# Attention heads: one PSUM bank of sums with two groups reopened in mid-head, four banks of scores, and fixed halves of rows

## The chip, the core and the metric

One core of a Trainium2 chip runs the whole program. Its engines are PE (matmuls; PEld is its weight load), DVE, ACT, POOL and SP; SP and ACT, and POOL for some, issue the DMAs. The metric is the device time in microseconds, lower is better.

## What is computed

Four layers in a row on 2048 tokens of 128 numbers. Each layer normalises, runs an attention and a feed-forward part, and adds their product to its input:

```python
xn = _layernorm(x, axis=-1)
s = _L0_attn_ref(xn, ...)            # layers 1, 2 and 3 likewise
g = _silu(_L0_ffn_ref(xn, ...))
x = x + s * g
```

The change touches the attentions of layers 0 and 3, with 16 heads of width 8 each. Layer 0's is full:

```python
scores = jnp.einsum('bhtd,bhsd->bhts', q, k) * scale
attn = jax.nn.softmax(scores, axis=-1)
out = jnp.einsum('bhts,bhsd->bhtd', attn, v)
```

Layer 3's is the same with rotated queries and keys and a causal mask (the reference takes 1e10 from a masked score, subtracts the row's maximum and takes the softmax).

## The kernel before

`attention_heads` runs both, `causal=False` for layer 0 (the full heads, some 50 to 750 us) and `causal=True` for layer 3 (the causal heads, some 1450 to 1922 us). Everything lies in stages; a stage ends with a barrier of all engines.

**Data of a head.** Queries and keys are split into three bf16 parts and stacked, with the products of parts that count, into 56 rows (`STK`) of `qs` and `ks`; this stack is loaded twice, into rows 0 to 55 and 64 to 119 (`HALF` is 64). Three rows more in each half (`qs`, rows 56 to 58 and 120 to 122) take the three parts of the negative row maxima, against rows of ones in `ks`. So a score matmul over 59 rows gives score minus maximum, and a maximum matmul over 56 rows gives the bare score. There are three sets of buffers (`ROUND`), head h in set h mod 3.

**Work of a head.** For a maximum, PE writes bare scores with queries on the partitions into a bank of `pM` (L742), and DVE reduces them (L880 in the full heads, two banks at once; L891 and, with the mask, L888 in the causal ones). When all are done, DVE makes `neg_max` (L897), its three parts are made (`split_max`, L610 to L616), PE transposes them (`turn`, L752) into a bank of `pS`, ACT copies them to `max_rows` (`keep_rows`, L836), and SP copies them into `qs` with one 4 KB DMA a part and half: six (`load_max_rows`, L643). For the result, PE writes scores with keys on the partitions into a bank of `pS` (L768; on the diagonal two 64-row mask matmuls follow, L771 and L772), ACT takes the exponential into `probs` (L855), and PE multiplies it by the values into 32-partition groups of `pO` (L786, the sums). ACT (full heads, L841) or DVE (causal, L910 and L911) copies `pO` to `ot`, and POOL stores it.

**Order.** It is written by hand, engine by engine. A head has units of four exponentials (`chunks`): 16 units in the full heads, 10 in the causal ones, where a unit pairs short and long rows of blocks. PE does the sums of unit u, and then the next four scores, each `RING` ahead of ACT, with the maxima of the next head (and of the one after) placed between them by `behind`. Scores wait for the bank that ACT freed `RING` chunks earlier, maxima for one of `FILLED` banks that DVE freed. Each matmul of L742 and L768 takes the other half of the rows than the one before it (`turns`), whatever it is:

```python
FILLED, RING, SUMS = (3, 3, 2) if causal else (4, 3, 1)
turns = itertools.cycle((0, HALF))
```

**Banks.** There are eight: full heads, four for maxima, three for scores, one for sums. Causal heads: three, three and two. Two, because in units 4 to 9 rows that lie behind the eighth or tenth are summed in groups that earlier units used for blocks 0 and 1 (`second`); those go to the second bank.

**Queues.** SP issues the loads of the head two on (`load_stacks`, ten DMAs, each behind a count of scores), then `load_max_rows`, then the row loads or clears of other work. At the start of a stage SP and ACT each load one half of the first keys (`load_first_keys`), SP behind DVE's first memset of ones and ACT behind its second. POOL sets the ones of the other two sets, two memsets each.

Of the kernel before, what the change touches and what calls it, by code (L numbers as in the profile page):

```python
# [18 lines left out]
P = 128  # L19
NT = T // P  # L20
BLK = 512
NB = T // BLK
# [73 lines left out]
def load_constants(nc, K, A):  # L96

    with Stage(nc, "load") as S:
# [17 lines left out]
        def _(dve):  # L116
# [9 lines left out]
            for to, at in ((slice(0, HALF), slice(HALF, P)), (slice(HALF, P), slice(0, HALF))):  # L126
                dve.tensor_copy(K.ident_swapped[to, :], K.ident[at, :]).then_inc(made, 1)
                dve.tensor_scalar(K.neg_below_swapped[to, :], masks[at, 1, :], NEG, None, ALU.mult).then_inc(made, 1)
# [388 lines left out]
def attention_heads(nc, K, layer, causal, scatter=None, spread=()):  # L517
# [11 lines left out]
    FILLED, RING, SUMS = (3, 3, 2) if causal else (4, 3, 1)  # L529
# [16 lines left out]
    with Stage(nc, f"heads{layer}") as S:  # L546
# [3 lines left out]
        ot = [S.sb(f"ot{i}", [P, SUMS, BLK]) for i in range(ROUND)]  # L550
# [10 lines left out]
        pO = S.ps("pO", [P, SUMS, BLK])  # L561
# [9 lines left out]
        last_stored = S.sem("last_stored")  # L571
        block = S.block()
# [3 lines left out]
        STORES = NB + len(SECOND)  # L576

# [27 lines left out]
        def split_max(queue, g):  # L605

            queue.wait_ge(splitting, 4 * g + 1)
            if g > 0:
                queue.wait_ge(rows_in, 32 * PARTS * g)
# [8 lines left out]
        def store_sums(queue, h, c, stored):  # L618
            for b in range(NB):
                queue.dma_start(K.head_out[h, :, b * BLK:(b + 1) * BLK], ot[c][b * 32:b * 32 + HD + 1, 0, :])\  # L620
                     .then_inc(stored, 16)
# [7 lines left out]
        def store_last(queue, turn):  # L629
            queue.wait_ge(ot_kept, LAST + 2)  # L630
            kept = ot[LAST % ROUND]
            pieces = [(K.head_out[LAST, :, b * BLK:(b + 1) * BLK], kept[b * 32:b * 32 + HD + 1, 0, :]) for b in range(NB)]
# [6 lines left out]
        def _(sp):  # L639
            def load_max_rows(c):  # L640
                for row in (STK, HALF + STK):
                    for a in range(PARTS):
                        sp.dma_start(qs[c % ROUND][row + a:row + a + 1, :].rearrange("o (t c) -> o t c", c=P),  # L643
                                     max_rows[a * NT:(a + 1) * NT, :]).then_inc(rows_in, 16)
# [16 lines left out]
            sp.wait_ge(ones_set[1], 2)  # L661
# [4 lines left out]
            sp.wait_ge(ones_set[2], 2)  # L666
# [12 lines left out]
        def _(pool):  # L679
# [7 lines left out]
            def one_head(p, c):  # L687
# [15 lines left out]
                if exists(p, c + 1):  # L703
                    pool.wait_ge(ot_kept, h + 2)
# [4 lines left out]
            for i in range(1, ROUND):  # L709
                for n, row in enumerate((HALF // 2, HALF + HALF // 2)):  # L710
                    pool.memset(ks[i][row:row + HALF // 2, :], 1.0).then_inc(ones_set[i], 1)
# [1906 lines left out]
```

## Time and profile before

| | us |
|---|---|
| median of 3 runs | 2002.25 |
| lowest, highest | 1996.25, 2002.73 |
| profiled execution | 1996.94 |
| its span, first to last instruction | 1995.1 |
| full heads, first maximum to last sums | 67 to 747 |
| causal heads, first maximum to last sums | 1466 to 1922 |

The page gives busy times over the whole span. The table by stretch gives them for a part of it; the granted clock 1.00 there is TensorE's upper level, 2.4 GHz, and 0.50 the lower, 1.2 GHz. The waits say who stood idle for whom, and the timeline gives rows in order: start, length, engine, line, what is written from what, how many in a row, and in brackets the idle time before them. Bursts of the same instruction are merged; their length is from the first start to the last end.

### The profile page before, as it was taken

To read this page: it belongs to the slowest core of one execution; us is meant where nothing else is said; L and a number is where in the kernel's file an instruction comes from. 1 tells how busy PE (TensorE), PEld (TensorE's weight loads), DVE (VectorE), ACT (ScalarE), POOL (GpSimd) and SP (SyncE) were. 2 spreads that over 40 slices of the span, in tenths; PEclk is the share of its full clock that TensorE was granted. 3 is DMA by queue.
4 is the path that set the end of the run, shared out by engine and by line. 5 is a ranking of instruction groups with operands and counts; after the bars stand their busy time and mean duration, and the time that the engine had idled before them with its cause. 6 is when DMAs were issued, how large, how long until landed. Compare 5 with 4: busy or idle time off the path is not lost. (4 is left out here: it accounts for less than half of the span.)

```text
span 1995.1 us, 29288 instructions
## 1 busy us (share of the span) xinstructions
PE 1650.5 (83%) x10105; PEld 666.2 (33%) x10105; DVE 1448.0 (73%) x2724; ACT 1112.2 (56%) x2262; POOL 313.7 (16%) x464
## 2 busy tenths in 40 slices
PE   3689999999999976799987986881659888999877
PEld 2212222222222214344444444771412222222246
DVE  5689999999999905855556056336768889999825
ACT  3258888888888881322212533342306666777744
POOL 0102100100010000000003345313012222111123
PEclk9779999999999997999987988886759999999989
DMA  4001111211110021063223587531501111111132
GB/s 132 32 20 63 66 51 45 73 61 46 46 61 32 4 47 66 5 127 94 93 105 112 154 285 252 184 114 49 182 33 46 47 41 45 42 45 52 32 78 69
DMA packets 80283, 156.07 MB, mean 78 GB/s; under 512 B 20476, under 2 KB 37756, under 8 KB 76440
## 3 DMA queue, kind: packets, MB, share of 16 engines
q1 hardware_dynamic: 65394, 123.90, 19.3%
q0 software_dynamic: 14384, 29.29, 4.9%
q8 instruction: 81, 1.33, 0.3%
q10 hardware_dynamic: 358, 1.01, 0.2%
q14 instruction: 66, 0.54, 0.1%
HBM read 104.33 MB, written 48.89 MB: 77 GB/s over the span
## 5 line engine op out<-in xcount | busy, mean ns | idle before, releaser
L855 ACT ACTIVATE heads_probs<-heads_pS 128x512 f32<-128x512 f32 (+3 forms) x1664 | 822.5, 578 | 217.9 <-PE heads_pS L768 195.5
L880 DVE TENSOR_REDUCE heads_run_max<-heads_pM 128x1 f32<-128x1024 f32 x512 | 601.0, 1219 | 37.0 <-PE heads_pM L742 29.1
L786 PE MATMUL heads_pO<-heads_probs,heads_vh 128*32 128x512 f32 (+2 forms) x3328 | 446.3, 583 | 2.1 <-ACT heads_probs L855 1.4
L768 PE MATMUL heads_pS<-heads_qs,heads_ks 59*128 59x512 bf16 (+3 forms) x1040 | 310.5, 371 | 30.4 <-ACT heads_probs L855 16.0
L742 PE MATMUL heads_pM<-heads_ks,heads_qs 56*128 56x512 bf16 (+3 forms) x1040 | 281.8, 380 | 17.3 <-DVE heads_run_max L891 7.1
L891 DVE TENSOR_REDUCE heads_run_max<-heads_pM 128x1 f32<-128x512 f32 x384 | 246.6, 684 | 18.9 <-PE heads_pM L742 17.8
L742 PE MATMUL heads_pM<-heads_ks,heads_q_first 56*128 56x512 bf16 x624 | 173.3, 397 | 44.1 <-DMA heads_ks<-k_parts_dram 25.8
L768 PE MATMUL heads_pS<-heads_q_first,heads_ks 59*128 59x512 bf16 x624 | 183.6, 376 | 23.8 <-ACT heads_probs L855 18.9
L768 PEld LDWEIGHTS heads_pS<-heads_qs,heads_ks 59*128 59x128 bf16 x1040 | 77.8, 94 | 321.6 <-ACT heads_probs L855 278.6
L888 DVE CUSTOM_DVE_ANT_0 heads_masked_out<-heads_pM,heads_mask_end 128x128 bf16<-128x128 f32 (+3 forms) x256 | 121.0, 486 | 28.5 <-PE heads_pM L742 26.1
L1616 DVE TENSOR_REDUCE second_row_max<-second_banks 128x1 f32<-128x2048 f32 (+15 forms) x16 | 20.7, 1291 | 156.0 <-PE second_banks L1574 77.5
L620 POOL DMA_DIRECT2D k_head_out_dram<-heads_ot x120 | 62.6, 529 | 365.3 <-DVE heads_ot L911 235.4
L1404 ACT ACTIVATE top_act_gate<-top_pG 128x512 f32<-128x512 f32 x68 | 40.6, 597 | 137.4 <-PE top_pU L1360 137.4
L768 PEld LDWEIGHTS heads_pS<-heads_q_first,heads_ks 59*128 59x128 bf16 x624 | 46.2, 94 | 201.8 <-ACT heads_probs L855 179.9
L1438 DVE TENSOR_TENSOR top_hidden<-top_act_gate,top_pU 128x512 f32<-128x512 f32 x68 | 46.7, 686 | 76.8 <-ACT top_act_gate L1404 76.8
L786 PEld LDWEIGHTS heads_pO<-heads_probs,heads_vh 128*32 128x32 f32 x3328 | 65.9, 108 | 96.3 <-issue 78.0
L742 PEld LDWEIGHTS heads_pM<-heads_ks,heads_qs 56*128 56x128 bf16 x1040 | 65.8, 94 | 96.3 <-DVE heads_run_max L880 62.6
L2115 POOL DMA_INDIRECT k_x_slots_dram<-k_xn,k_place_i x32 | 31.1, 971 | 390.3 <-DVE k_place_i L1984 361.5
L742 PEld LDWEIGHTS heads_pM<-heads_ks,heads_q_first 56*128 56x128 bf16 x624 | 39.7, 94 | 106.6 <-DVE heads_run_max L880 48.8
L610 POOL CAST heads_max_parts<-heads_neg_max 128x16 bf16<-128x16 f32 x16 | 3.1, 196 | 458.0 <-DVE heads_neg_max L897 458.0
L1359 PE MATMUL top_pG<-k_xnT,k_gate 128*128 128x512 f32 x128 | 67.3, 608 | 4.2 <-PEq L68 4.2
L1368 PE MATMUL top_pY<-top_hidden,k_down 128*128 128x512 f32 x128 | 65.7, 594 | 1.6 <-DVE top_hidden L1444 1.6
(384 smaller groups left out, 2139.5 us busy)
## 6 DMA issues: line engine op xcount, KB each, us to landing
top_weights<-k_comb_dram SPq DMA_DIRECT2D x128, 128.0 KB, 3.0
second_w<-in_L_W_dram SPq DMA_DIRECT2D x12, 1024.0 KB, 10.0
heads_ks<-k_parts_dram SPq DMA_DIRECT2D x124, 96.0 KB
k_hid_slots_dram<-k_zeros SPq DMA_DIRECT2D x8, 1152.0 KB, 4.5
k_h_slots_dram<-second_work SPq DMA_DIRECT2D x48, 192.0 KB
second_work<-k_hid_slots_dram SPq DMA_DIRECT2D x48, 192.0 KB
heads_qs<-k_parts_dram SPq DMA_DIRECT2D x40, 192.0 KB
k_parts_dram<-proj_part SPq DMA_DIRECT2D x12, 512.0 KB, 4.7
```

The source lines that it names most:

```text
L620: queue.dma_start(K.head_out[h, :, b * BLK:(b + 1) * BLK], ot[c][b * 32:b * 32 + HD + 1, 0, :])\
L742: mm = pe.matmul(pM[:, bank_of(c, j, k), 0:w], qs[c % ROUND][rows, i * P:(i + 1) * P], ks[c % ROUND][rows, b * BLK:b * BLK + w], start=Tru ...
L768: mm = pe.matmul(pS[:, slot, 0:c1 - c0], ks[c % ROUND][rows, u * P:(u + 1) * P], qs[c % ROUND][rows, c0:c1], start=True, stop=not diag)
L786: mm = pe.matmul(pO[k * 32:k * 32 + VW, int(second), o:BLK], vh[c][:, t, :], probs[u % 2][:, k * BLK + o:(k + 1) * BLK], start=first_chunk ...
L855: act.activation(probs[u % 2][:, k * BLK + c0 - b * BLK:(k + 1) * BLK], pS[:, slot, 0:c1 - c0], ACT.Exp)\
L880: dve.reduce_max(run_max[:, i, blocks[0][0] // 2:blocks[0][0] // 2 + 1], both.rearrange("p k c -> p (k c)"), AX.X).then_inc(taken, 2)
L888: dve.tensor_tensor_reduce(masked_out[:, i % TPB, 0:w], pM[:, bank, 0:w], mask_end[:, BLK - w:BLK], 1.0, LOWEST, ALU.add, ALU.max, run_max ...
L891: dve.reduce_max(run_max[:, i, b:b + 1], pM[:, bank, 0:w], AX.X).then_inc(taken, 1)
L1359: pe.matmul(pG[:, m % 2, :], gw, x, start=True, stop=True)
L1368: pe.matmul(pY[:, b % 2, :], w, hidden[:, m % 2, :], start=(n == 0), stop=(n == L1_J)).then_inc(downed, 1)
L1404: act.activation(act_gate[:, m % 2, :], pG[:, m % 2, :], ACT.Silu).then_inc(gated, 1)
L1438: mix = dve.tensor_tensor(hidden[:, m % 2, :], act_gate[:, m % 2, :], pU[:, m % 2, :], ALU.mult)
```

## The change

- **Banks, causal heads only.** `pO` has one bank, `pS` four (`RING` 4). The group of block 0 is complete when the sums of unit 3 are done, that of block 1 after unit 7. ACT copies each (32 partitions, 512 columns) to `ot` before it goes on with the third exponential of unit 4 and of unit 8; PE waits for that copy (`early_kept`) before the sums of that unit, which open the group again. At the head's end DVE copies the one bank with one instruction instead of two banks with two. POOL's stores also wait for `early_kept`.
- **Halves, both kinds of head.** `turns` is gone. Scores and masks use rows 0 to 63, maxima rows 64 to 127. So the maxima's rows are copied into the lower half alone: three DMAs instead of six. The stacks are still loaded into both halves.
- **Starts, both.** The upper half needs no ones: one DVE memset instead of two, two on POOL instead of four, and ACT's loads of the first keys wait for nothing.
- **The turn.** `TURN_AT` is `first_chunk[7] + RING`, so in the causal heads ACT copies the rows of the maxima behind chunk 31 instead of chunk 30.

```diff
-    FILLED, RING, SUMS = (3, 3, 2) if causal else (4, 3, 1)
+    FILLED, RING, KEPT = (3, 4, 2) if causal else (4, 3, 1)
...
+        reopened = {k: min(u for u, pieces in enumerate(units) if pieces[k][4]) for k, _ in SECOND}
+        EARLY = len(reopened)
+        keep_at = {first_chunk[u] + 2: k for k, u in reopened.items()}
...
         def load_first_keys(queue, turn):
             half = (0, HALF)[turn]
-            queue.wait_ge(ones_set[0], turn + 1)
+            if half == 0:
+                queue.wait_ge(ones_set[0], 1)
...
-                for row in (STK, HALF + STK):
-                    for a in range(PARTS):
-                        sp.dma_start(qs[c % ROUND][row + a:row + a + 1, :].rearrange("o (t c) -> o t c", c=P),
-                                     max_rows[a * NT:(a + 1) * NT, :]).then_inc(rows_in, 16)
+                for a in range(PARTS):
+                    sp.dma_start(qs[c % ROUND][STK + a:STK + a + 1, :].rearrange("o (t c) -> o t c", c=P),
+                                 max_rows[a * NT:(a + 1) * NT, :]).then_inc(rows_in, 16)
...
-                    at = next(turns)
-                    rows = slice(at, at + STK)
+                    rows = slice(HALF, HALF + STK)
...
-                at = next(turns)
-                rows, mask = slice(at, at + STK + PARTS), slice(at, at + HALF)
+                rows, mask = slice(0, STK + PARTS), slice(0, HALF)
...
+                opened = [k for k in reopened if reopened[k] <= u]
+                if u in reopened.values():
+                    pe.wait_ge(early_kept, EARLY * h + len(opened))
...
-                    mm = pe.matmul(pO[k * 32:k * 32 + VW, int(second), o:BLK], vh[c][:, t, :],
+                    mm = pe.matmul(pO[k * 32:k * 32 + VW, o:BLK], vh[c][:, t, :],
...
+                    if n in keep_at:
+                        rows = slice(keep_at[n] * 32, (keep_at[n] + 1) * 32)
+                        act.wait_ge(used, NU * h + 2 + reopened[keep_at[n]])
+                        act.activation(ot[c][rows, 0, :], pO[rows, :], ACT.Copy).then_inc(early_kept, 1)
...
-                        dve.tensor_copy(ot[c][:, 0, :], pO[:, 0, :])
-                        dve.tensor_copy(ot[c][0:2 * 32, 1, :], pO[0:2 * 32, 1, :]).then_inc(ot_kept, 1)
+                        dve.tensor_copy(ot[c][:, 1, :], pO[:, :]).then_inc(ot_kept, 1)
```

ACT in a causal head, from the exponentials of unit 3 to those of unit 8. `heads_probs<-heads_pS` is an exponential, `heads_max_rows` the copy of the maxima rows. Before:

```order
376 L855 ACTIVATE heads_probs<-heads_pS 128x512 x7
377 L855 ACTIVATE heads_probs<-heads_pS 128x384 x2
378 L855 ACTIVATE heads_probs<-heads_pS 128x512 x2
379 L855 ACTIVATE heads_probs<-heads_pS 128x256 x2
380 L855 ACTIVATE heads_probs<-heads_pS 128x512 x2
381 L855 ACTIVATE heads_probs<-heads_pS 128x128 x2
382 L855 ACTIVATE heads_probs<-heads_pS 128x512
383 L836 ACTIVATE heads_max_rows<-heads_pS 48x128
384 L855 ACTIVATE heads_probs<-heads_pS 128x512 x3
```

And after, in the same head:

```order
379 L865 ACTIVATE heads_probs<-heads_pS 128x512 x5
380 L858 ACTIVATE heads_ot<-heads_pO 32x512
381 L865 ACTIVATE heads_probs<-heads_pS 128x512 x2
382 L865 ACTIVATE heads_probs<-heads_pS 128x384 x2
383 L865 ACTIVATE heads_probs<-heads_pS 128x512 x2
384 L865 ACTIVATE heads_probs<-heads_pS 128x256 x2
385 L865 ACTIVATE heads_probs<-heads_pS 128x512 x2
386 L865 ACTIVATE heads_probs<-heads_pS 128x128 x2
387 L865 ACTIVATE heads_probs<-heads_pS 128x512 x2
388 L842 ACTIVATE heads_max_rows<-heads_pS 48x128
389 L865 ACTIVATE heads_probs<-heads_pS 128x512 x2
390 L858 ACTIVATE heads_ot<-heads_pO 32x512
```

The two copies of sums stand after the second exponential of units 4 and 8, and the copy of the maxima rows one exponential later than before.

PE in a causal head, from the last score ahead of the sums of unit 0 to the scores and maxima behind them (`heads_pO` the sums, `heads_pM` a maximum, `k_neg_below` the masks). Before:

```order
2416 L768 MATMUL heads_pS<-heads_qs,heads_ks 128x512
2417 L742 MATMUL heads_pM<-heads_ks,heads_qs 128x256
2418 L768 MATMUL heads_pS<-heads_qs,heads_ks 128x512
2419 L786 MATMUL heads_pO<-heads_probs,heads_vh 32x512 x4
2420 L768 MATMUL heads_pS<-heads_qs,heads_ks 128x512
2421 L742 MATMUL heads_pM<-heads_ks,heads_qs 128x512
2422 L768 MATMUL heads_pS<-heads_qs,heads_ks 128x256
2423 L771 MATMUL heads_pS<-k_neg_below,k_ident_b 128x128
2424 L772 MATMUL heads_pS<-k_neg_below_swapped,k_ident_swapped 128x128
```

And after, at the same place:

```order
2416 L771 MATMUL heads_pS<-heads_qs,heads_ks 128x512
2417 L746 MATMUL heads_pM<-heads_ks,heads_qs 128x256
2418 L771 MATMUL heads_pS<-heads_qs,heads_ks 128x512
2419 L792 MATMUL heads_pO<-heads_probs,heads_vh 32x512 x4
2420 L771 MATMUL heads_pS<-heads_qs,heads_ks 128x256
2421 L774 MATMUL heads_pS<-k_neg_below,k_ident_b 128x128
2422 L775 MATMUL heads_pS<-k_neg_below_low,k_ident_low 128x128
2423 L746 MATMUL heads_pM<-heads_ks,heads_qs 128x512
```

Every score stands one place further ahead of its sums; the maxima have kept their places.

## Rows read from the trace of the kernel before

**Rows 1.** The page: busy us, share of the span and instructions.

```profile
PE 1650.5 (83%) x10105; PEld 666.2 (33%) x10105; DVE 1448.0 (73%) x2724; ACT 1112.2 (56%) x2262; POOL 313.7 (16%) x464
```

**Rows 2.** Busy time by stretch: length, PE, PEld, DVE, ACT, POOL, clock, DMA.

```profile
150.00:390.00 240.00, 232.81 (x1567) 54.03 (x1559) 230.60 (x202) 205.86 (x403) 28.75 (x58) 1.00 0.16 56
...
1517.60:1708.15 190.55, 166.32 (x1353) 53.80 (x1351) 168.62 (x442) 130.27 (x287) 51.60 (x77) 0.98 0.15 45
...
1708.15:1889.95 181.80, 163.92 (x1348) 53.72 (x1346) 166.64 (x437) 129.51 (x287) 25.15 (x50) 1.00 0.15 43
```

**Rows 3.** Waits from 150 to 700 us; then DVE in order of time.

```profile
DVE heads_run_max L880 <- PE heads_pM L742: 11.9, 31, 0.8
...
317.75 2.36 DVE L880 TENSOR_REDUCE heads_run_max<-heads_pM 128x1 f32<-128x1024 f32 x2 [0.44 <-PE heads_pM L742]
...
501.16 2.36 DVE L880 TENSOR_REDUCE heads_run_max<-heads_pM 128x1 f32<-128x1024 f32 x2 [0.39 <-PE heads_pM L742]
...
633.74 19.09 DVE L880 TENSOR_REDUCE heads_run_max<-heads_pM 128x1 f32<-128x1024 f32 x16 [0.23 <-PE heads_pM L742]
```

**Rows 4.** SP's queue in order of time; the copies' landing.

```profile
309.85 4.28 SPq L643 DMA_DIRECT2D heads_qs<-heads_max_rows  x6
...
623.65 3.71 SPq L643 DMA_DIRECT2D heads_qs<-heads_max_rows  x6
...
1543.55 6.56 SPq L643 DMA_DIRECT2D heads_qs<-heads_max_rows  x6
...
1734.11 3.72 SPq L643 DMA_DIRECT2D heads_q_first<-heads_max_rows  x6
...
DMA to landing us min/median/max: 1.6/1.7/5.0
```

**Rows 5.** Starts of both stages in order of time; causal chain; page's DMA issues.

```profile
54.59 2.15 SPq L603 DMA_DIRECT2D heads_ks<-k_parts_dram  x3
...
56.85 1.97 ACTq L603 DMA_DIRECT2D heads_ks<-k_parts_dram  x3
...
67.16 1.04 PE L742 MATMUL heads_pM<-heads_ks,heads_q_first 56*128 56x512 bf16 x4 [4.81 <-DMA heads_ks<-k_parts_dram]
...
1457.99 7.59 DMA heads_ks<-k_parts_dram
...
top_weights<-k_comb_dram SPq DMA_DIRECT2D x128, 128.0 KB, 3.0
```

**Rows 6.** Head 15 of the causal stage, ACT and PE in order of time.

```profile
1904.45 2.06 ACT L855 ACTIVATE heads_probs<-heads_pS 128x512 f32<-128x512 f32 x4 [0.65 <-PE heads_pS L768]
...
1905.42 1.06 PE L786 MATMUL heads_pO<-heads_probs,heads_vh 128*32 128x128 f32 x8
...
1906.84 1.85 ACT L855 ACTIVATE heads_probs<-heads_pS 128x512 f32<-128x512 f32 x4 [0.33 <-PE heads_pS L768]
```

**Rows 7.** Copies of the sums by line: duration ns min/median/max.

```profile
L841 ACT ACTIVATE heads_ot<-heads_pO x16: 597/602/604, 159.6 to 746.1; 128x512 f32<-128x512 f32 x16
...
L911 DVE COPY heads_ot<-heads_pO x16: 672/673/674, 1525.9 to 1921.2; 64x512 f32<-64x512 f32 x16
```

**Rows 8.** A later causal head in order of time, PE and DVE.

```profile
1739.01 0.39 PE L768 MATMUL heads_pS<-heads_q_first,heads_ks 59*128 59x512 bf16 x1
...
1739.17 0.69 DVE L891 TENSOR_REDUCE heads_run_max<-heads_pM 128x1 f32<-128x512 f32 x1 [0.84 <-PE heads_pM L742]
```

**Rows 9.** The same head, matmuls in one half; page's weight loads of scores.

```profile
1736.82 0.27 PE L768 MATMUL heads_pS<-heads_qs,heads_ks 59*128 59x256 bf16 x1
...
1736.98 0.21 PE L772 MATMUL heads_pS<-k_neg_below_swapped,k_ident_swapped 64*128 64x128 bf16 x1
...
L768 PEld LDWEIGHTS heads_pS<-heads_qs,heads_ks 59*128 59x128 bf16 x1040 | 77.8, 94 | 321.6 <-ACT heads_probs L855 278.6
```

**Rows 10.** PE in the first full head; waits from 1517 to 1709 us.

```profile
103.19 0.61 PE L742 MATMUL heads_pM<-heads_ks,heads_q_first 56*128 56x512 bf16 x2 [0.52 <-DVE heads_run_max L880]
...
PE heads_pS L768 <- DMA heads_qs<-heads_max_rows: 5.7, 3, 2.7
```

More of the change, by code:

```diff
@@ L124, in _ @@
             dve.tensor_scalar(K.neg_below[:, :], masks[:, 1, :], NEG, None, ALU.mult).then_inc(made, 1)
-            for to, at in ((slice(0, HALF), slice(HALF, P)), (slice(HALF, P), slice(0, HALF))):
-                dve.tensor_copy(K.ident_swapped[to, :], K.ident[at, :]).then_inc(made, 1)
-                dve.tensor_scalar(K.neg_below_swapped[to, :], masks[at, 1, :], NEG, None, ALU.mult).then_inc(made, 1)
+            dve.tensor_copy(K.ident_low[:, :], K.ident[HALF:P, :]).then_inc(made, 1)
+            dve.tensor_scalar(K.neg_below_low[:, :], masks[HALF:P, 1, :], NEG, None, ALU.mult).then_inc(made, 1)
 class Norm:
@@ L549, in attention_heads @@
         vh = [S.sb(f"vh{i}", [P, NT, VW]) for i in range(ROUND)]
-        ot = [S.sb(f"ot{i}", [P, SUMS, BLK]) for i in range(ROUND)]
+        ot = [S.sb(f"ot{i}", [P, KEPT, BLK]) for i in range(ROUND)]
         probs = [S.sb(f"probs{i}", [P, T]) for i in range(2)]
@@ L576, in attention_heads, with sums_of_block @@
         STORES = NB + len(SECOND)
+        reopened = {k: min(u for u, pieces in enumerate(units) if pieces[k][4]) for k, _ in SECOND}
+        EARLY = len(reopened)
+        keep_at = {first_chunk[u] + 2: k for k, u in reopened.items()}
+        def sums_of_block(kept, b):
+            return kept[b * 32:b * 32 + HD + 1, 1 if causal and b not in reopened else 0, :]
         def every_head(one_head):
@@ L608, in split_max @@
             if g > 0:
[L609 removed]
+                queue.wait_ge(rows_in, 16 * PARTS * g)
             queue.tensor_copy(max_parts[:, 0, :], neg_max[:, :]).then_inc(splitting, 1)
@@ L629, in store_last @@
         def store_last(queue, turn):
+            queue.wait_ge(early_kept, EARLY * HEADS)
             queue.wait_ge(ot_kept, LAST + 2)
             kept = ot[LAST % ROUND]
-            pieces = [(K.head_out[LAST, :, b * BLK:(b + 1) * BLK], kept[b * 32:b * 32 + HD + 1, 0, :]) for b in range(NB)]
+            pieces = [(K.head_out[LAST, :, b * BLK:(b + 1) * BLK], sums_of_block(kept, b)) for b in range(NB)]
             pieces += [(K.head_more[LAST, :, (b - 2) * BLK:(b - 1) * BLK], kept[k * 32:k * 32 + HD + 1, 1, :])
@@ L709, in _ @@
             for i in range(1, ROUND):
-                for n, row in enumerate((HALF // 2, HALF + HALF // 2)):
-                    pool.memset(ks[i][row:row + HALF // 2, :], 1.0).then_inc(ones_set[i], 1)
-                    pool.wait_ge(ones_set[i], n + 1)
+                pool.memset(ks[i][HALF // 2:HALF, :], 1.0).then_inc(ones_set[i], 1)
+                pool.wait_ge(ones_set[i], 1)
             for i in range(ROUND):
@@ L725, in _ @@
         def _(pe):
-            turns = itertools.cycle((0, HALF))
             def bank_of(c, j, k):
@@ L771, in score_chunk @@
                     pe.matmul(pS[:, slot, 0:P], K.ident_b[mask, :], K.neg_below[mask, :], start=False, stop=False)
-                    mm = pe.matmul(pS[:, slot, 0:P], K.ident_swapped[mask, :], K.neg_below_swapped[mask, :], start=False,
+                    mm = pe.matmul(pS[:, slot, 0:P], K.ident_low[:, :], K.neg_below_low[:, :], start=False,
                                    stop=True)
@@ L914, in one_head @@
                             take(p, c + d, j)
-            for row in (HALF // 2, HALF + HALF // 2):
-                dve.memset(ks[0][row:row + HALF // 2, :], 1.0).then_inc(ones_set[0], 1)
+            dve.memset(ks[0][HALF // 2:HALF, :], 1.0).then_inc(ones_set[0], 1)
             if causal:
```

30 lines of the change are left out of this document (16 added, 14 removed).

## The prediction

> **What bounds the kernel now.** I read the page's busy shares first [rows 1], then the table by stage [rows 2], then the waits and the order of time inside the two stages that the change touches. Over the whole span no engine is the bound: PE, the busiest, has 83% [rows 1]. By stage it is clearer. In the full heads (150 to 699 us) DVE works 230.60 of 240 us [rows 2]: its 32 maxima a head run back to back, and what interrupts them is a group of short idles at each change of head, 11.9 us in 31 waits for maxima matmuls [rows 3]. In the causal heads from 1708 to 1890 us seven heads take 181.80 us, 25.97 each, and DVE is busy for 23.81 of them, PE for 23.42, ACT for 18.50 [rows 2]. No engine is full; the period comes from a loop. In head 15, where no maxima are made, ACT starts its four exponentials every 2.39 us (1904.45, 1906.84) and is idle 0.33 to 0.65 us before them [rows 6]: with three banks, the last score before the sums of a unit needs the bank that the unit's last exponential frees, the sums (1.06 us, at 1905.42) stand behind it in PE's order, and the first score behind the sums is what ACT then waits for.
>
> **Changes of head in the full heads.** SP issues six 4 KB copies of the maxima rows: 4.28 us where a code fetch or a clear is near, 3.71 us elsewhere, and the last needs 1.7 us to land [rows 4]. Behind the slow issue at 309.85 DVE is idle for 0.44 us at 317.75, and once more; behind the quick one at 623.65 there is one idle of 0.23 us, at 633.74 [rows 3, 4]: the excess follows the slow issue. Three copies need half the issue, about 1.9 us, at worst with the same excess of 1.3 us, 3.2 us: less than the 3.71 us that already do no harm. Taken off: 11.9, less two waits of 0.39 that lie in mid-head (one at 501.16 [rows 3]) and fourteen of 0.23 that stay, 7.9 us (7 to 9). SP's queue is only relieved: stack loads and clears stand behind the copies and move forward.
>
> **Starts of the two stages.** ACT's three loads of the first keys now wait for a second DVE memset: issued at 56.85 for 1.97 us, and PE starts 4.81 us late, at 67.16, on a load [rows 5]. In the causal stage ACT's last load is issued at 1457.99 and lands 7.59 us later [rows 5]. That wait is gone, so ACT's loads leave at the stage's start and SP's three, issued from 54.59 to 56.74 [rows 5], land last. No row has their landing. Bounds: 3.0 us (128 KB, a quiet time) and 7.59 us (three queues' worth in flight) [rows 5], so the first maximum at 59.7 to 64.3 instead of 67.16: 2.8 to 7.4 us. With half of the traffic already gone I take 5 us, and the same for the causal stage, whose start has the same shape: 10 us (6 to 13). Four memsets fewer on POOL and two on DVE are beside this wait.
>
> **Fixed halves.** Scores now always stream from rows 0 to 63, maxima from 64 to 127, and two neighbours in one half can't overlap. In the steady loops the neighbours are nearly always one of each; where the full heads have M M and S S next to each other, the pairs that start together (S M, M S, S M, M S) are those of before, so nothing is lost. The first head of a stage is all maxima: a pair takes 0.61 us with PE idle 0.52 us before it [rows 10]; one behind the other adds 512 columns at the low clock (1.2 GHz, 0.43 us), which leaves almost no slack in DVE's 1.13 us. I add 1.7 us for both first heads (0 to 3). In head 15 scores alone follow each other, 0.21 us each, inside the time of ACT's exponentials: nothing.
>
> The row for back-to-back matmuls of one half: a 256-column score starts at 1736.82, and the second mask matmul behind it, after 384 columns of the same half, at 1736.98 [rows 9]: 0.16 us, the streaming alone at 2.4 GHz. The Trainium skill (TensorE: Matmul & The Clock Gate, Part 3: Packing small matmuls) says that a weight load overlaps a running matmul only when it goes to other rows of the array; by that every such neighbour would cost its load, and this trace does not agree.
>
> **Causal heads, the copied rows.** The same six copies took 6.56 us at 1543.55 and 3.72 us in the later heads [rows 4]; PE waited up to 2.7 us for them [rows 10]. The seven heads from 1517.60 to 1708.15 took 190.55 us, 8.8 us over seven times 25.97 [rows 2]. Three copies halve that issue, but the turn now stands one exponential later, and what fetches SP's code can still hit it. I take 5.9 us of the 8.8 (3 to 8.8). In the later heads SP's issue begins at 1734.11 and PE takes the next head's first score at 1739.01 [rows 4, 8], 4.9 us against 3.1 + 1.7: just in time. After: 1.3 + 1.7 = 3.0 us against about 3.9 (0.6 less for the later turn, 0.4 for a faster loop).
>
> **Causal heads, the loop.** With four banks one more score stands ahead of the sums, so ACT has four exponentials (2.06 us) to do while PE does 0.4 + 1.0 + 0.33 us: ACT no longer waits and the loop of 2.39 opens. PE then needs 1.06 us of sums, four times 0.21 us of score and maximum side by side, 0.17 us of masks (16 a head, two each) and about 0.1 us of hand-over: 2.2 us a unit, 22 a head. DVE drops its second copy (0.67 us, [rows 7]): 23.81 - 0.67 = 23.1 us a head. That is the floor. Of DVE's 2.2 idle us a head some stay, since the maxima are spread unevenly: three behind unit 7 and five behind unit 8, where it waits 0.84 us now [rows 8]; I leave 1.0.
>
> Then the two added copies, each a new wait: ACT stops after two exponentials of the unit until the sums of the unit before are done, copies 32 rows (nearest row: 128 rows of the same 512 columns, 0.602 us [rows 7]; between nothing and that), and only then come the last two exponentials, behind which PE waits. Sums to sums: 1.0 + 0.1 + 0.5 + 1.1 + 0.2 = 2.9 us instead of 2.3. Behind PE's wait stand scores and maxima, behind those DVE, with three banks (1.8 us) in hand. So 0 to 0.8 us each; I take 0.35 for both, since most falls under DVE's work. Period 23.1 + 1.0 + 0.35 = 24.5 us, 1.47 less. Fifteen heads: 22 us. Bounds: 23.1 (43 us) and 25.97 (nothing). Head 15 gains 0.2 a unit and pays two copies: nothing.
>
> **Sum.** 7.9 + 10 - 1.7 + 5.9 + 22 = 44 us. The profiled execution took 1996.94 us (span 1995.1), so 1953; the median of the three runs is 2002.25, 5.3 above it, so 1958.
>
> **Rivals.**
> 1. The loop opens fully. DVE runs at its floor of 23.1 us: 21 us more, 1937. For it: DVE is the fullest engine. Against: the three-maxima unit.
> 2. The mid-head copies take it back. Each costs PE its full 0.6 to 0.8 us and DVE follows, so the period stays at 25.9: 1980. For it: PE at 22 of 24.5 us has little to catch up with, and one copy falls right behind the thin unit 7. Against: three banks of maxima.
> 3. Loads bound the faster loop. The keys for two heads on, and the rows, land as late as before while PE asks earlier: period 25.2, 1958 + 10 = 1968. For it: the margins above are within a microsecond.
> 4. The slower side: weight loads in one half are exposed. There are 720 such neighbours in the full heads (three a unit) and about 150 in the causal ones. At a load's 0.094 us each [rows 9] they cost 82 us: 1958 + 82 = 2040. It decides from 0.05 us a neighbour. Against it stand the 0.16 us of [rows 9]. The Trainium skill's rule above would have it so.
> 5. The change doesn't do what it says at the starts, because the loads landing last are SP's own and take 7.59 us: 6 us less, 1964; inside the range of the forecast.
>
> **Chances.** Forecast 0.45 with 5 (1948 to 1968), rival 1 0.15, rival 2 0.2, rival 3 0.15, rival 4 0.05. The range takes in rivals 1 to 3 and the bounds of the load landing: 1936 to 1984. A measurement of this kernel can tell 0.3% (6 us) from no change: faster 0.92, same 0.04, slower 0.04.
>
> **What would show it.** In the full heads: DVE idle 0.23 at each change of head, period near 38.7 us. At the starts: first maxima near 62 and 1461. In the causal heads: turns 24.5 us apart, ACT's wait before its fours gone except at the two copies, DVE busy 95% of a head. Wrong would be: a turn distance of 25.9 with PE waiting for the copied rows of the sums (rival 2); PE waiting on key loads (3); scores of one half 0.3 us apart instead of 0.21 (4).

## The result and the profile after

The changed kernel takes 1989.46 us (median of 5 runs, 1981.55 to 1991.0) against 2002.25 for the kernel before beside it: ratio 0.9937 (0.9917 to 0.9957). It is faster, by 0.6% where the prediction had 2.2%, and lies above its range (1936 to 1984 us). The span of the profiled executions fell from 1995.1 to 1989.2 us.

The table by stretch of the changed kernel, from 150 to 390 us in the full heads and for two stretches of the causal ones, six and seven heads from one copy of maxima rows to another (length, PE, PEld, DVE, ACT, POOL, granted clock, DMA share, GB/s):

```profile
150.00:390.00 240.00, 239.56 (x1601) 57.28 (x1598) 235.10 (x206) 210.14 (x412) 28.45 (x56) 1.00 0.17 61
1536.73:1698.35 161.62, 141.28 (x1160) 44.89 (x1159) 141.59 (x373) 116.81 (x258) 44.36 (x66) 1.00 0.15 45
1698.35:1885.80 187.45, 164.48 (x1349) 52.14 (x1348) 163.90 (x432) 136.29 (x302) 25.26 (x50) 1.00 0.14 41
```

The full heads are what was forecast: DVE busy 235.10 of 240 us, 230.60 before [rows 2]. The causal heads are not: seven take 187.45 us, **26.78 each**, where they took 25.97 [rows 2] and 24.5 was forecast. DVE and PE have 23.4 and 23.5 us of work in them, so both stand idle longer than before.

Some of the waits of the changed kernel from 1517 to 1880 us (us in total, times, longest):

```profile
ACT heads_probs L865 <- PE heads_pS L775: 59.0, 68, 1.3
...
ACT heads_ot L858 <- PE heads_pO L792: 27.1, 27, 1.3
...
DVE heads_run_max L901 <- PE heads_pM L746: 19.0, 13, 2.2
```

The second row is new: ACT waits at each mid-head copy for the sums of the unit before, 1.0 us on average. The third was 13.0 us in 16 waits, the longest 0.8, in the same view of the kernel before. In order of time, ACT in one causal head (start, length, and in brackets the idle time before; `heads_ot` is the mid-head copy):

```profile
1645.08 1.08 ACT L865 ACTIVATE heads_probs<-heads_pS 128x512 f32<-128x512 f32 x2
1647.46 0.59 ACT L858 ACTIVATE heads_ot<-heads_pO 32x512 f32<-32x512 f32 x1 [1.29 <-PE heads_pO L792]
1648.07 2.40 ACT L865 ACTIVATE heads_probs<-heads_pS 128x384 f32<-128x384 f32 x6
...
1661.69 1.08 ACT L865 ACTIVATE heads_probs<-heads_pS 128x512 f32<-128x512 f32 x2 [0.87 <-PE heads_pS L775]
1663.52 0.59 ACT L858 ACTIVATE heads_ot<-heads_pO 32x512 f32<-32x512 f32 x1 [0.75 <-PE heads_pO L792]
1664.02 4.49 ACT L865 ACTIVATE heads_probs<-heads_pS 128x512 f32<-128x512 f32 x10
```

Units 8 and 4: two exponentials, 1.29 and 0.75 us idle, the copy of 0.59 us, then the other exponentials. The third exponential starts 3.0 and 2.3 us after the first instead of 1.0, and PE's later scores of the next unit, which need the banks that the last two exponentials free, and the sums stand behind them.

The starts and the changes of head of the changed kernel, the same rows as [rows 3 to 5]:

```profile
59.62 1.02 PE L746 MATMUL heads_pM<-heads_ks,heads_q_first 56*128 56x512 bf16 x4 [1.72 <-DMA heads_ks<-k_parts_dram]
...
652.73 1.82 SPq L649 DMA_DIRECT2D heads_qs<-heads_max_rows  x3
...
DVE heads_run_max L890 <- PE heads_pM L746: 3.3, 14, 0.2
...
1458.10 1.79 PE L746 MATMUL heads_pM<-heads_ks,heads_q_first 56*128 56x128 bf16 x6 [16.35 <-DMA heads_ks<-k_parts_dram]
```

The first maximum comes at 59.62 us instead of 67.16, and fourteen changes of head (the third row, from 150 to 735 us) hold one idle of at most 0.2 us each. The two profiles differ by 5.9 us:

| stretch | before, us | after, us | difference |
|---|---|---|---|
| to the first full maximum | 67.16 | 59.62 | -7.5 |
| maxima of the first full head | 39.40 | 45.45 | +6.1 |
| the second full head | 42.51 | 43.29 | +0.8 |
| fourteen further full heads | 549.81 | 540.75 | -9.1 |
| from there to the first causal maximum | 766.84 | 768.99 | +2.2 |
| first causal head, to the first copy of rows | 22.79 | 22.78 | 0.0 |
| fifteen causal heads | 401.14 | 404.92 | +3.8 |
| last causal head and the rest | 105.45 | 103.40 | -2.1 |

### The profile page after: what moved, and what is told of

It is laid out like the page before. It is cut to its first block and busy times, and to the rows that moved or that the text cites. A ratio compares the mean times of both kernels' runs of the same rounds, so it can differ in the third digit from the quotient of the medians.

```text
span 1989.2 us, 29248 instructions
## 1 busy us (share of the span) xinstructions
PE 1678.2 (84%) x10105; PEld 672.3 (34%) x10105; DVE 1437.9 (72%) x2704; ACT 1127.3 (57%) x2294; POOL 306.7 (15%) x460
## 5 line engine op out<-in xcount | busy, mean ns | idle before, releaser
L746 PE MATMUL heads_pM<-heads_ks,heads_qs 56*128 56x512 bf16 (+3 forms) x1040 | 319.0, 379 | 19.9 <-DVE heads_run_max L901 9.6
L746 PE MATMUL heads_pM<-heads_ks,heads_q_first 56*128 56x512 bf16 x624 | 201.4, 397 | 33.8 <-DMA heads_ks<-k_parts_dram 18.1
L771 PE MATMUL heads_pS<-heads_q_first,heads_ks 59*128 59x512 bf16 x624 | 189.9, 377 | 13.2 <-ACT heads_probs L865 11.8
L898 DVE CUSTOM_DVE_ANT_0 heads_masked_out<-heads_pM,heads_mask_end 128x128 bf16<-128x128 f32 (+3 forms) x256 | 121.2, 487 | 25.9 <-PE heads_pM L746 21.6
L1870 PE MATMUL second_banks<-second_w,second_hT 128*96 128x128 f32 x384 | 56.1, 294 | 15.6 <-ACT second_hT L1921 8.6
```

The costliest lines, as they stand in the source:

```text
L746: mm = pe.matmul(pM[:, bank_of(c, j, k), 0:w], qs[c % ROUND][rows, i * P:(i + 1) * P], ks[c % ROUND][rows, b * BLK:b * BLK + w], start=Tru ...
L771: mm = pe.matmul(pS[:, slot, 0:c1 - c0], ks[c % ROUND][rows, u * P:(u + 1) * P], qs[c % ROUND][rows, c0:c1], start=True, stop=not diag)
L898: dve.tensor_tensor_reduce(masked_out[:, i % TPB, 0:w], pM[:, bank, 0:w], mask_end[:, BLK - w:BLK], 1.0, LOWEST, ALU.add, ALU.max, run_max ...
L1870: pe.matmul(pY[0:R, n % 2, 0:D], hT[:, n % 2, f, :], w[:, e, f * D:(f + 1) * D], start=(f == 0), stop=False)
```

## The experiments

Two questions: what made the causal heads slower than before, and what took the start's gain back. Theory A puts the first down to the two mid-head copies and the waits around them; B to the fixed halves; C to the end of a head. All experiments were measured later, each beside the kernel before, which takes 1946 to 1948 us there: the stages between the two kinds of heads are some 50 us shorter (672.2 us in one more profile of it instead of 719.6). The record names two chips for them, 12 (`copy_latest`, `dve_copies`, `again`, `later_alt`) and 0 (the others). So they are compared by ratio, and by the causal period: the mean distance of the copies of maxima rows in the late heads, a head with a stall left out. For one and the same kernel the period agrees in all measurements (25.97 and 25.96 us before, 26.78 and 26.79 after).

**1. `two_banks`: all of the change but the banks** (and what hangs on them: the mid-head copies, the later turn, DVE's one copy instead of two)**.**

```diff
-    FILLED, RING, KEPT = (3, 4, 2) if causal else (4, 3, 1)
+    FILLED, RING, KEPT = (3, 3, 2) if causal else (4, 3, 1)
...
-        pO = S.ps("pO", [P, BLK])
+        pO = S.ps("pO", [P, KEPT, BLK])
...
-        keep_at = {first_chunk[u] + 2: k for k, u in reopened.items()}
+        keep_at = {}
...
```

> The changed kernel with the sums as before: two banks of sums and three of scores in the causal heads, no copy in mid-head, two copies by DVE at a head's end. Fixed halves, three copies of rows and the early loads stay. In the changed kernel the maxima rows of the causal heads are copied every 26.8 us (26.0 in the kernel before). Theory A, the two mid-head copies and their waits cost it: here the period is the loop of the kernel before, 25.9 us, without its stalls behind six row copies, so 15 x 0.9 = 13.5 us less than the changed kernel, some of it given back in head 15 (2.8 us): 1979 us. Theory B, PE loses by the fixed halves in the loop: the period stays at 26.8 or above, 1990 us or more. Theory C, the end of a head (turn, rows, first scores) sets the period whatever the banks: 26.0 to 26.8.

Measured: 1927.42 us, ratio 0.9892 (0.9872 to 0.9912), where the changed kernel had 0.9937. Period 25.95 us against 25.97. Fixed halves cost nothing in the loop, and B falls: the new period comes with the banks. C's lower bound of 26.0 is too near to 25.95 to be ruled out by this run alone; the next one does that.

**2. `no_copies`: the changed kernel without ACT's copies and PE's waits for them.**

```diff
-        keep_at = {first_chunk[u] + 2: k for k, u in reopened.items()}
+        keep_at = {}
...
-                if u in reopened.values():
-                    pe.wait_ge(early_kept, EARLY * h + len(opened))
```

> The changed kernel without the two mid-head copies and PE's waits for them: the sums of blocks 0 and 1 of the causal heads are therefore overwritten and wrong, all else is as in the changed kernel (one bank of sums, four of scores). Theory A (the copies and their waits cost the gain of the fourth bank): period 24.5 us, 15 x 2.3 = 34 us less than the changed kernel, 1955 us. Theory B (fixed halves): period 26 at least, 1977 us. Theory C (end of head): 26.0 to 26.8 here too, 1980 to 1989.

Measured: 1900.94 us, ratio 0.9774 (0.9750 to 0.9799), period 24.91. This kernel has the same end of head as the changed one, later turn included, so C falls. Seven of its heads in the table by stretch:

```profile
1603.29:1777.64 174.35, 161.74 (x1353) 52.35 (x1352) 163.12 (x435) 129.47 (x287) 29.27 (x54) 1.00 0.16 49
```

The fourth bank (with the later turn and DVE's one copy less) is worth 25.95 - 24.91 = 1.04 us a head, and the mid-head copies with their waits cost 26.79 - 24.91 = 1.9. DVE works 23.3 of the 24.91 us: 1.6 us idle stay where the prediction left 1.0.

Where the 1.9 us go shows in PE's rows from the sums of unit 7 to those of unit 8, first in the changed kernel, with the copy of 1647.46 between them, then without copies:

```profile
1646.35 1.06 PE L792 MATMUL heads_pO<-heads_probs,heads_vh 128*32 128x128 f32 x8
...
1648.62 0.23 PE L771 MATMUL heads_pS<-heads_qs,heads_ks 59*128 59x128 bf16 x1 [0.66 <-ACT heads_probs L865]
...
1649.42 1.06 PE L792 MATMUL heads_pO<-heads_probs,heads_vh 128*32 128x512 f32 x8
```

```profile
1629.79 1.07 PE L789 MATMUL heads_pO<-heads_probs,heads_vh 128*32 128x128 f32 x8
...
1631.72 1.06 PE L789 MATMUL heads_pO<-heads_probs,heads_vh 128*32 128x512 f32 x8
```

From sums to sums it is 3.07 us with the copy and 1.93 without; from unit 3 to unit 4 it is 3.04 and 2.32. The two differences, 1.14 and 0.72, add up to the 1.9 us: nothing of them is hidden. The third exponential comes behind the copy, PE waits 0.66 us for the bank that it frees before it writes its third score, and the maxima, the last score and the sums stand behind that one. DVE then waits 1.4 us for the maxima behind the sums of unit 8, where it waits 0.5 us without copies (the 2.2 of the view further up is from one early head).

**3. `copies_ring3`: the changed kernel with three banks of scores.**

```diff
-    FILLED, RING, KEPT = (3, 4, 2) if causal else (4, 3, 1)
+    FILLED, RING, KEPT = (3, 3, 2) if causal else (4, 3, 1)
```

> The changed kernel with three banks of scores instead of four; one bank of sums and the two mid-head copies stay (one bank of PSUM unused). Theory A: the fourth bank is worth 25.9 - 24.5 = 1.4 us a head and the copies cost 2.3 us, so without it the period is 28.2 us, 21 us more than the changed kernel: 2010 us. If the mid-head wait makes the fourth bank worthless, since PE refills it only behind the same sums, the period stays at 26.8: 1989 us. Theory C: also 26.8.

Measured: 1942.0 us, ratio 0.9979 (0.9967 to 0.9991), period 27.18. So with the copies in that place the fourth bank is worth only 0.4 us a head, not 1.04. The distance from sums to sums over a copy is 3.03 and 3.04 us here and 3.07 and 3.04 with four banks, where without copies it is 2.34 and 2.40 with three banks (`two_banks`) and 1.93 and 2.32 with four: the copy sets it, and what the bank opens in these two units is lost. Neither number forecast (28.2 or 26.8) was met.

**4 and 5. `copy_later` and `copy_latest`: the same copies behind the third and behind the fourth exponential.** One number is changed, to 3 in `copy_later` and to 4 in `copy_latest`:

```diff
-        keep_at = {first_chunk[u] + 2: k for k, u in reopened.items()}
+        keep_at = {first_chunk[u] + 4: k for k, u in reopened.items()}
```

> The changed kernel with each mid-head copy one exponential later: behind the third exponential of units 4 and 8 instead of the second. ACT waited 1.3 us for the sums of the unit before ahead of each copy; with one exponential (0.52 us) more in front the wait is 0.8 us, and PE gets the copy no later. Theory A: up to 2 x 0.5 = 1.0 us a head less, period 25.8 to 26.3, 1975 to 1982 us. If PE then waits as much longer for the copy as ACT waits less, nothing changes: 1989 us. Theories B and C: nothing, 1989 us.

> The changed kernel with each mid-head copy behind all four exponentials of units 4 and 8 (second in the changed kernel, third gave 25.92 us a head). ACT finds the sums done and waits no more (0.6 us less for each than behind the third); but PE's sums of the unit come only after the copy, 0.6 us later. Theory: each costs about its own 0.6 us in front of PE's sums, 24.91 + 1.2 = 26.1 us a head, between the other two; 1918 us. If PE has room there, 25.3.

Measured: behind the third 1915.13 us, ratio 0.9839 (0.9821 to 0.9857), period 25.92; behind the fourth 1903.45 us, ratio **0.9777** (0.9758 to 0.9795), period **24.91**, the same as with no copy at all. The miss on the last is over 1 us a head. ACT of that kernel in order of time, units 4 and 8:

```profile
1646.51 2.06 ACT L865 ACTIVATE heads_probs<-heads_pS 128x512 f32<-128x512 f32 x4 [0.87 <-PE heads_pS L775]
1648.43 0.58 ACT L858 ACTIVATE heads_ot<-heads_pO 32x512 f32<-32x512 f32 x1
1648.91 1.81 ACT L865 ACTIVATE heads_probs<-heads_pS 128x384 f32<-128x384 f32 x4
...
1655.97 1.96 ACT L865 ACTIVATE heads_probs<-heads_pS 128x512 f32<-128x512 f32 x4
1658.33 0.59 ACT L858 ACTIVATE heads_ot<-heads_pO 32x512 f32<-32x512 f32 x1 [0.39 <-PE heads_pO L792]
```

In unit 4 the sums are long done when ACT comes, and the copy takes 0.5 us of its time. In unit 8 it still waits 0.39 us, but the kernel without copies stands idle there too, 0.72 us before the next unit's exponentials and 0.51 us before those behind them:

```profile
1631.21 1.53 ACT L862 ACTIVATE heads_probs<-heads_pS 128x512 f32<-128x512 f32 x4 [0.72 <-PE heads_pS L770]
1633.26 2.06 ACT L862 ACTIVATE heads_probs<-heads_pS 128x512 f32<-128x512 f32 x4 [0.51 <-PE heads_pS L774]
```

Wait and copy take 0.98 us, and the two idles hold them. My expectation for the fourth place (26.1 us, since PE's sums come only after the copy) was wrong for PE as well: the unit's own exponentials no longer wait for the copy, so the banks that they free come as early as without it, and PE is still at its scores and maxima when the copy ends, at 1658.92; its sums start at 1659.14, 1.93 us behind those of unit 7, as without copies. The distance from the exponentials of unit 4 to those of unit 8 is 1671.88 - 1661.69 = 10.19 us in the changed kernel and 1655.97 - 1646.51 = 9.46 in `copy_latest`; from unit 8 to the next unit 4 it is 16.61 and 15.44. So by this count too the copy of unit 4 cost 0.7 us and that of unit 8 1.2.

**6. `dve_copies`: the copies on DVE, ahead of its maxima of units 4 and 8.**

```diff
-                    if n in keep_at:
...
+                    for k in [k for k in reopened if causal and reopened[k] == u]:
+                        rows = slice(k * 32, (k + 1) * 32)
+                        dve.wait_ge(used, NU * h + 2 + u)
+                        dve.tensor_copy(ot[c][rows, 0, :], pO[rows, :]).then_inc(early_kept, 1)
```

> The changed kernel with the two mid-head copies on DVE instead of ACT, ahead of its maxima of units 4 and 8 (0.6 us each). Theory A (the cost of 1.9 us a head lies in ACT's wait for the sums, behind which the exponentials and then PE's next sums stand): DVE waits for maxima that come behind the same sums anyway, ACT never stops; DVE's work is 23.1 + 1.2 = 24.3 us a head, period 24.9 to 25.5, 15 x 1.6 = 24 us below the changed kernel, 1910 us. Rival: what costs is that PE's sums and banks wait for any copy, or that DVE, the fullest engine, pays every copy in full on top of 24.9: 26.1 us, 1923.

Measured: 1985.3 us, ratio 1.0201 (1.0182 to 1.0221), period 30.5, heads between 29.0 and 32.6 us. A miss by 5 us a head. Of its timeline, DVE's copy, PE's sums behind it, the sets behind those, and the granted clock by stretch of a short and a long head:

```profile
1646.37 0.68 DVE L917 COPY heads_ot<-heads_pO 32x512 f32<-32x512 f32 x1
1647.20 1.35 PE L792 MATMUL heads_pO<-heads_probs,heads_vh 128*32 128x512 f32 x8 [1.83 <-DVE heads_ot L917]
...
1649.34 2.06 ACT L861 ACTIVATE heads_probs<-heads_pS 128x512 f32<-128x512 f32 x4 [3.01 <-PE heads_pS L775]
1649.38 0.69 DVE L897 TENSOR_REDUCE heads_run_max<-heads_pM 128x1 f32<-128x512 f32 x1 [2.32 <-PE heads_pM L746]
```

```profile
1612.80:1641.81 29.01, 23.23 (x195) 7.59 (x193) 24.61 (x65) 18.46 (x42) 7.36 (x11) 1.00 0.14 41
1641.81:1674.37 32.56, 27.46 (x195) 8.19 (x193) 24.69 (x65) 18.72 (x42) 7.37 (x11) 0.84 0.12 37
```

The sums that the copy waits for are done at 1644.44, but DVE runs up to three banks of maxima behind PE, and its copy stands behind them, at 1646.37. So PE waits 1.83 us, until DVE has caught up, then DVE waits 2.32 us for PE and ACT 3.01 us: all three engines are brought to a stop together. At 1647.86 the granted clock falls to the lower level for 6.8 us, in the middle of PE's eight sums, which take 1.35 us instead of 1.06; the head before, where PE waits 1.83 and 2.09 us for the copies, stays at 1.00. How much of the 5.6 us a head the clock costs wasn't separated, but the heads at 1.00 take 29.0 us, 4.1 more than without copies. A copy on POOL, which is busy for 7.4 us of such a head, wasn't tried: the Trainium skill (PSUM — Partial Sum Buffer, The four PSUM rules) says that POOL has no way to PSUM, and no run here shows it.

**7. `again`: the changed kernel once more, and `before_again`, one profile of the kernel before, beside the experiments.**

> The changed kernel once more, beside the variants on the same chip. The copies of maxima rows of the causal heads 26.8 us apart and the full heads 38.62 us, as in its first profile. By its first ratio (0.994) 1934 us beside 1946 for the kernel before; but the variants with the same full heads lay 3.8 us above (copies in mid-head, three banks, ratio 0.998: 15 x 0.4 us more in the causal heads), so 1936. If the 7 us that the changed kernel lost between the two kinds of heads in the first profile belong to the change, its causal stage begins later here than in copy_later (first causal maximum at 1398.9 us); if not, at the same time within 2 us.

> The kernel before once more, for its profile on the chip of the variants. In the first profiles the stages between the two kinds of heads (last copied sums of the full heads to first causal maximum, the start of the causal stage included) took 719.6 us before and 721.7 after; on the second chip the changed kernel and its variants took 665.4 to 669.0. If the change's earlier loads bring the causal stage 5 us and nothing else there depends on the change, this run shows 670 to 674; if the change costs time between the stages, 660 to 666. Full heads: first maxima 39.4 us (1.2 GHz or not, two halves), 39.3 us a head; causal heads 26.0 us apart late, with stalls before.

Measured: 1931.25 us, ratio 0.9927 (0.9908 to 0.9946), period 26.79: the first result repeats. From the last copied sums of the full heads to the first causal maximum the kernel before needs 672.2 us here, and the two kernels with its late loads (10 and 11) 674.7 and 670.1; the changed one needs 665.4 and the eight variants with its early loads 666.2 to 669.0. So the change gains about 5 us there, as forecast for the start of the stage. The 7 us that the first profile lost between the stages (719.6 against 721.7, with those 5 gained in it) don't come back, and no run ties them to the change. Some 5 us of them went between 1207 and 1287 us of the kernel before, where the code of the two kernels is the same: the same DVE instruction (`second_row_max`) comes 8.4 us earlier in the changed kernel at the first time and 3.1 us earlier at the second. What delayed the work there is open.

**8 and 9. The first full head: `later_alt` and `latest_alt`.** Its maxima took 39.40 us before and 45.45 after. The table by stretch of `before_again`, `again` and `two_banks` from 60 to 75 us (the kernel before makes its first maximum only at 65.59):

```profile
60.00:75.00 15.00, 11.51 (x46) 4.74 (x45) 7.74 (x7) 3.19 (x6) 0.28 (x1) 0.80 0.16 64
...
60.00:75.00 15.00, 14.09 (x76) 7.83 (x76) 11.86 (x11) 3.45 (x6) 0.00 (x0) 1.00 0.15 57
...
60.00:75.00 15.00, 15.00 (x40) 6.85 (x38) 8.84 (x8) 1.79 (x3) 0.00 (x0) 0.50 0.13 48
```

With fixed halves these 15 us hold eleven DVE instructions at a granted clock of 1.00 (2.4 GHz) and eight at 0.50 (1.2 GHz), with PE busy for 14.1 and 15.0 of them. The maxima of the first head, as in the changed kernel, took 41.5 us where the stretch ran at 1.00 (five runs, stage starts at 51.4 to 52.2 us), 45.5 at 0.66 (two runs, starts at 50.6 and 50.7) and 48.5 at 0.50 (one run, 50.6). `later_alt` is `copy_later`, `latest_alt` is `copy_latest`, each with the maxima of a stage's first head by turns in the two halves again; they need no copied rows, so three DMAs stay enough.

```diff
-                    rows = slice(HALF, HALF + STK)
+                    half = HALF if not (p == 0 and c == 0) or (before[j] + k) % 2 == 0 else 0
+                    rows = slice(half, half + STK)
```

> The kernel with the mid-head copy behind the third exponential, and the maxima of a stage's first head taking turns between the two halves again (they need no rows of ones or maxima, so three row copies stay enough). Theory: the first full head's maxima took 41.5 to 48.3 us (39.4 in the kernel before) since four 512-column matmuls in one half follow each other at 1.2 GHz (1.9 to 2.1 us against 1.04); with turns they take 38.7 to 39.5 us again, 2 to 6 us less: 1911 us beside 1915. If the chip's clock alone set it, the first head stays at 41.5.

> The changed kernel with the two mid-head copies behind the fourth exponential of units 4 and 8 and the maxima of a stage's first head in both halves by turns. The copies gave 24.91 us a head there, as without any copy, and turns took 2 to 3 us off the first full head: 1903.5 - 2.5 = 1901 us, ratio 0.976 to the kernel before. If the turns only shift when the clock falls and rises, 1903.

PE's maxima at 1.2 GHz in `again` and in `later_alt`:

```profile
93.42 2.17 PE L746 MATMUL heads_pM<-heads_ks,heads_q_first 56*128 56x512 bf16 x4 [0.26 <-DVE heads_run_max L890]
...
93.48 0.60 PE L747 MATMUL heads_pM<-heads_ks,heads_q_first 56*128 56x512 bf16 x2 [0.52 <-DVE heads_run_max L891]
```

Four in one half take 2.17 us and come 2.42 apart with the wait, 1.21 us a pair; two in two halves take 0.60 and come every 1.13. The first head takes 38.5 us in both kernels (59.51 to 97.98, 60.76 to 99.23), 3.0 less than the 41.5 at the same clock; the second head may give part of it back (43.6 and 43.9 us, where the five runs had 42.9 three times and 43.8 and 43.9 once each). Whole time: 1913.23 us, ratio 0.9830 (0.9810 to 0.9850), for `later_alt`, 0.9839 without turns; and **1900.55 us, ratio 0.9746** (0.9721 to 0.9772), for `latest_alt`, the lowest of all, 0.9777 (0.9758 to 0.9795) without turns. Neither total tells the kernel from the one without turns; the gain is shown in the first head alone.

**10 and 11. The banks alone, in the kernel before.** `banks_only` puts one bank of sums, four of scores and the copies behind the second exponential into the kernel before, with halves by turns, six row copies and late loads; `banks_only_latest` has the copies behind the fourth.

```diff
-    FILLED, RING, SUMS = (3, 3, 2) if causal else (4, 3, 1)
+    FILLED, RING, KEPT = (3, 4, 2) if causal else (4, 3, 1)
...
+        keep_at = {first_chunk[u] + 2: k for k, u in reopened.items()}
```

> The kernel before with the change of banks alone: in the causal heads one bank of sums, four of scores, ACT's copies behind the second exponential of units 4 and 8, one copy by DVE at the end. Halves by turns, six row copies, ones in both halves and the late loads stay as before. Theory: the changed kernel's period of 26.8 us comes from this part, so 15 x 0.8 = 12 us slower than the kernel before in the loop, some of the row stalls (11.6 us in all) hidden behind it, 2.8 us back in the last head: 1950 to 1956 beside 1946. Rival: the loss came from fixed halves with four banks (with three banks they cost nothing): period 25.9 or below, 1940 or less.

> As banks_only, with each mid-head copy behind the fourth exponential. Theory: 24.9 us a head as in copy_latest, 15 x 1.05 = 16 us less than the kernel before, less or more by what six row copies do to a faster loop: turn to next scores needs 5.4 us with six and 3.0 with three. 1928 to 1938 us. If the rows bind, the period is 25.5 or more.

Measured: `banks_only` 1957.27 us, ratio **1.0048** (1.0032 to 1.0064), period 26.78, the same as in the changed kernel with its fixed halves. `banks_only_latest` 1947.74 us, ratio 0.9997 (0.9979 to 1.0015), where 1928 to 1938 was forecast; undisturbed heads are 25.6 us apart, not 24.9, and six between 27.0 and 29.8. Its waits from 1466 to 1860 us, and the copies in SP's queue ahead of a wait of 2.62 us that ends at 1741.28:

```profile
PE heads_pS L778 <- DMA heads_qs<-heads_max_rows: 15.8, 10, 3.1
...
PE heads_pS L778 <- DMA heads_q_first<-heads_max_rows: 5.3, 5, 2.8
```

```profile
1734.41 3.72 SPq L651 DMA_DIRECT2D heads_qs<-heads_max_rows  x6
```

PE waits 21.1 us in 15 waits for the copied rows; in `copy_latest`, with three row copies, it is 1.5 us in two waits. An undisturbed head has one such wait, 0.64 us at 1768.47, and is 0.7 us longer than one of `copy_latest`. So the faster loop needs the three copies: with six, the rows come last, and the opened loop brings nothing (the fifteen causal heads take 403.1 us, 403.6 in `before_again`).

## Why the prediction was wrong, point by point

The forecast was 44 us less and the profiles differ by 5.9. Of the 38 us between, 34 lie in one term, the causal loop.

- **Full-head boundaries, -7.9.** Right: fourteen heads 9.1 us faster, 38.62 us each, one idle of 0.2 us at each change of head, copies issued in 1.82 us.
- **Starts, -10.** Right in size. The first full maximum came 7.5 us earlier, 2.1 of them since the stage itself began earlier (DVE's first memset of ones at 50.73 instead of 52.80), which is no part of the change and was luck, 5.4 from the loads. The causal start brought 5.1, from the first memset to the first maximum (13.3 us before, 8.2 after). Rival 5, with its landing of 7.59 us, would by the prediction's own bounds cost 10 - 2 x 2.8 = 4.4 us, not 6.
- **First heads, +1.7 (0 to 3).** Mis-sized: +6.1 in the first full head, +0.8 in the second, nothing in the first causal one (21.3 us in both). At 1.2 GHz the prediction had 0.61 + 0.43 = 1.04 us for a pair in one half, still under DVE's 1.13; measured 1.21 with the wait, 0.08 more than 1.13. What I left out is that steps of the feed-forward part run between the same maxima (PE is busy for 14.93 of the 15 us from 60 to 75), and that the clock of that stretch differs from run to run: at the same clock the halves cost 3.0 us, 41.5 against 38.5.
- **Causal row stalls, -5.9 of 8.8.** Right: over fifteen heads what exceeds the late period fell from 401.14 - 15 x 25.97 = 11.6 to 404.92 - 15 x 26.78 = 3.2 us, 8.4 less.
- **The causal loop, -22.** The step that failed: +12.2 us (15 x 0.81). Two terms of it. The opened loop: 24.1 us forecast without the copies (23.1 + 1.0), 24.91 measured, since DVE works 23.3 us and keeps 1.6 idle. And the mid-head copies: 0.35 us for both, from a range of 0 to 0.8 each, "since most falls under DVE's work". Measured 1.9 us for both, 0.72 and 1.14 from sums to sums, above the upper end of 1.6. The chain that I had written down, sums to sums 2.9 us, was right: 3.07 and 3.04 measured. Two things were wrong with what I made of it. First, it replaces not 2.3 us but 2.32 in one unit and 1.93 in the other, where the fourth bank had opened the loop, so the price by the chain itself was 0.6 and 1.0, not 0.6 each. Second, nothing of it fell under DVE's work: the third score waits for the delayed exponential, the maxima stand behind that score, and DVE, instead of covering the delay out of its three banks, waits 1.4 us a head at unit 8 where it waits 0.5 without the copies.
- **Head 15, nothing.** It and the rest brought 2.1 us.
- **Rivals.** The second one happened, and more than it said: 26.8 us instead of 25.9, by which it would have been 1980 + 15 x 0.9 = 1994, against 1989; what kept the total below that is the other terms. Its "0.6 to 0.8 us" fits the copy of unit 4 (0.7) and not that of unit 8, behind the thin unit 7 that it named. Rival 4, exposed weight loads, is refuted by `two_banks`: with all scores in one half and all maxima in the other the period is 25.95, and the full heads, with 720 such neighbours by the prediction's count, became faster. The rule of the Trainium skill that I named for it (TensorE: Matmul & The Clock Gate, Part 3: Packing small matmuls) doesn't show in this loop's time. Rival 3 was right about where the next bound lies as far as the rows go, but for a kernel with six row copies.
- **What the change is worth by parts** (ratios of the experiments): all but the banks 0.9892; the banks alone 1.0048; both 0.9927. The banks, the part that was to bring half of the gain, make the kernel slower with the copies in that place, and the changed kernel is faster by its other parts.

## What to carry to other kernels

Where an engine is made to wait in the middle of its own sequence, its place decides more than the work that is added: the same 0.59 us copy cost 0.9 us on average behind the second exponential, 0.5 behind the third and nothing behind the fourth. There the engine stands idle in any case, before the copy or soon behind it, and the other engine doesn't need yet what stands behind the copy. Look in the trace for such a place. When you price a wait, take the distance that it replaces from the loop as it will be, not as it is, and don't count on another engine's work to hide it before you have seen what that engine itself waits for. Don't put such a copy on an engine that runs behind by several buffers: its whole backlog comes before it. And when a loop gets faster, price again what was just in time: six row copies cost the late heads nothing at 25.97 us a head, and took the whole gain of the loop that is 24.9 us long with three.

## What the runs showed of the hardware that was not expected

- A copy of 32 partitions and 512 columns from PSUM takes as long as one of 128: 0.59 us on ACT against 0.60 [rows 7], 0.68 us on DVE against 0.67 for 64 partitions [rows 7].
- The first head's time depends on the granted clock in the stretch that it begins in: 41.5, 45.5 or 48.5 us for the same instructions at 1.00, 0.66 and 0.50 from 60 to 75 us. With fixed halves the three runs that began their stage earliest (50.6 to 50.7 us, the others 51.4 to 52.2) had the lower clock; why, no run here shows. With maxima in two halves it was 39.1 to 39.4 us at 0.77 and 0.80, and 38.5 at 1.00.
- In `dve_copies`, where PE, ACT and DVE come to a stop twice a head (PE for 1.8 and 2.1 us), the granted clock fell again and again in the causal heads: 0.84 over the head shown, 0.89 over all of them. In the late heads of the other kernels it was 1.00, but for one head of `banks_only_latest` that waited for its rows (0.94).
